# POOL interleaves its gathers and scatters in pairs in a mixture-of-experts kernel

## The reference

```python
x = x + 0.5 * ffn(layernorm(x))
x = x + attn(layernorm(x))
x = x + 0.5 * ffn(layernorm(x))

def ffn(h):                        # the part that the change touches
    probs = softmax(h @ gate_W.T)              # 8 experts
    top_v, top_i = top_k(probs, 2)             # each token takes two
    gates[t, top_i[t]] = top_v[t]
    out_e = (silu(h @ w1_e) * (h @ w3_e)) @ w2_e   # 128 -> 512 -> 128, for each expert
    routed = sum over e of gates[:, e] * out_e[e]
    shared = (mean over 8 small experts of the same form)
    return 0.5 * shared + 0.5 * routed
```

## Time and profile before

| | |
|---|---|
| median of 3 runs | 809.28 us |
| lowest, highest | 808.66, 810.8 us |
| span of the profiled execution | 936.1 us |
| mean granted clock of TensorE in it | 0.937 of full speed |
| PE busy | 733.7 us, 78% |
| POOL busy | 453.4 us, 48% |
| indirect DMAs | 144 fetches, 144 sends |

### The profile page before, as it was taken

One profiled execution on the slowest core, in us unless ns is written; L12 is line 12 of the kernel. 1 busy time (PEld: TensorE's weight loads), 2 busy tenths in 40 slices (PEclk: granted clock), 3 DMA queues, 4 the chain that ended last, 5 costly groups with the idle time before them and its releaser, 6 DMA issues. The chain is left out here.

```text
span 936.1 us, 16201 instructions
## 1 busy us (share of the span) xinstructions
PE 733.7 (78%) x4308; PEld 601.7 (64%) x4309; DVE 453.9 (48%) x1108; ACT 341.4 (36%) x889; POOL 453.4 (48%) x580
## 2 busy tenths in 40 slices
PE   4878979787878888937877689899878887978850
PEld 3757768676767676824654577687757666767740
DVE  7697633332233232426999847653324232333327
ACT  3514613323232332437764253633223233232320
POOL 6780054464535455358886240033554545546433
PEclk9979989998999999968999899999999999999985
DMA  9500010010111111031101000000110101111127
GB/s 329 173 1 1 1 35 29 29 39 28 39 28 34 34 34 34 26 98 47 45 24 35 23 23 1 1 23 24 32 37 28 39 28 39 34 34 36 31 68 224
DMA packets 45126, 43.68 MB, mean 47 GB/s; under 512 B 6048, under 2 KB 39840, under 8 KB 44704
## 3 DMA queue, kind: packets, MB, share of 16 engines
q1 hardware_dynamic: 31648, 22.22, 7.7%
q0 software_dynamic: 9216, 18.89, 7.3%
q10 hardware_dynamic: 4224, 2.10, 0.8%
HBM read 27.46 MB, written 15.73 MB: 46 GB/s over the span
## 5 line engine op out<-in xcount | busy, mean ns | idle before, releaser
L1073 ACT ACTIVATE silu<-psG 128x512 f32<-128x512 f32 x208 | 123.7, 596 | 330.4 <-PE psG L1206 210.1
L714 DVE TENSOR_TENSOR hr<-silu,psU 128x512 f32<-128x512 f32 x144 | 98.9, 687 | 282.5 <-ACT silu L1073 136.2
L1357 PE MATMUL psY<-W,hT 128*128 x1120 | 158.9, 287 | 26.9 <-issue 16.8
L602 POOL DMA_INDIRECT results<-yout,target_now x144 | 141.0, 979 | 63.9 <-issue 35.2
L583 POOL DMA_INDIRECT rows<-tokens,source_now x144 | 138.7, 963 | 58.6 <-issue 38.3
L1357 PEld LDWEIGHTS psY<-W,hT 128*128 128x128 f32 x1120 | 141.9, 199 | 38.2 <-issue 38.1
L1116 ACT ACTIVATE hT<-psH 128x512 f32<-128x512 f32 x144 | 85.9, 597 | 118.9 <-PE psH L1340 74.2
L1340 PE MATMUL psH<-ident,hr 128*128 128x128 f32 x576 | 89.7, 279 | 42.4 <-DVE hr L714 39.1
L1340 PEld LDWEIGHTS psH<-ident,hr 128*128 128x128 f32 x576 | 69.8, 142 | 73.2 <-ACT hT L1116 24.9
L1204 PE MATMUL psG<-W13H,xTH 128*128 x144 | 72.6, 504 | 15.4 <-issue 6.8
L579 POOL COPY source_now<-source 128x4 int32 (+1 forms) x36 | 7.0, 195 | 141.0 <-DVE source L866 117.7
(11 more groups left out here) (177 smaller groups left out, 1306.3 us busy)
## 6 DMA issues: line engine op xcount, KB each, us to landing
W<-w_e SPq DMA_DIRECT2D x3, 2048.0 KB, 13.8
tokens<-XN SPq DMA_DIRECT2D x16, 256.0 KB, 3.1
Y<-results SPq DMA_DIRECT2D x32, 128.0 KB, 2.2
YF<-results SPq DMA_DIRECT2D x16, 256.0 KB, 5.3
rows<-tokens,source_now POOLq DMA_INDIRECT x144
results<-yout,target_now POOLq DMA_INDIRECT x144
X<-x SPq DMA_DIRECT2D x8, 256.0 KB, 5.6
out<-X ACTq DMA_DIRECT2D x8, 256.0 KB, 2.6
```

The lines of the kernel that those rows point to most:

```text
L602: pool.indirect_dma_start(results, bass.IndirectOffsetOnAxis(ap=target_now[:, s.u, t:t + 1], axis=0), yout[:, s.u, t, :], None).then_inc(y ...
L714: dve.tensor_tensor(hidden, silu[:, s.u % 2, :], psU[:, s.u % 2, :], ALU.mult).then_inc(h_done, 1)
L1073: act.activation(silu[:, s.u % 2, :], psG[:, s.u % 2, :], ACT.Silu).then_inc(silu_done, 1)
L1357: i = pe.matmul(into[:, t * D:(t + 1) * D], hT[:, s.u % 2, f, :], W2[:, bass.ds(at + f * D, D)], start=(f == 0), stop=(f == FT - 1))
```

## The change

The two stages of POOL's pipeline are each cut in two halves, and the halves alternate. A step k is now: wait for `y_done` of group k - 3, copy its targets, two sends; wait for the buffer of group k, copy its sources, two fetches; the other two sends; the other two fetches. Nothing else in the kernel changes.

```diff
-                def fetch_rows(s):
-
-                    if s.past(2):
-                        wait_apart(pool, xT_psum, s.i + (l * GROUPS - 1))
-                    pool.tensor_copy(source_now[:, s.u, :], source[:, bass.ds(s.i * GT, GT)])\
-                        .then_inc(source_link, 1)
-                    wait_apart(pool, source_link, s.i + (l * GROUPS + 1))
-                    for t in range(GT):
-                        pool.indirect_dma_start(
...
-                pipelined(pool, [(fetch_rows, 0), (send_results, 3)], GROUPS, 2, guard=1)
+                def fetch_pair(half):
+                    def run(s):
+                        if half == 0:
+                            if s.past(2):
+                                wait_apart(pool, xT_psum, s.i + (l * GROUPS - 1))
+                            pool.tensor_copy(source_now[:, s.u, :], source[:, bass.ds(s.i * GT, GT)])\
+                                .then_inc(source_link, 1)
+                            wait_apart(pool, source_link, s.i + (l * GROUPS + 1))
+                        for t in range(half * GT // 2, (half + 1) * GT // 2):
+                            pool.indirect_dma_start(
...
+                def send_pair(half):
+                    def run(s):
+                        last = isinstance(s.i, int) and s.i == GROUPS - 1
+                        if half == 0:
+                            if not last:
+                                wait_apart(pool, y_done, s.i + (l * GROUPS + 1))
...
+                        for t in range(half * GT // 2, (half + 1) * GT // 2):
...
+                pipelined(pool, [(send_pair(0), 3), (fetch_pair(0), 0), (send_pair(1), 3), (fetch_pair(1), 0)],
+                          GROUPS, 2, guard=1)
```

More of the change, by code:

```diff
@@ L573, in _ @@
                 pool.wait_ge(table_done, l + 1)
-                def fetch_rows(s):
-                    if s.past(2):
-                        wait_apart(pool, xT_psum, s.i + (l * GROUPS - 1))
-                    pool.tensor_copy(source_now[:, s.u, :], source[:, bass.ds(s.i * GT, GT)])\
-                        .then_inc(source_link, 1)
-                    wait_apart(pool, source_link, s.i + (l * GROUPS + 1))
-                    for t in range(GT):
-                        pool.indirect_dma_start(
-                            rows[:, s.u, t, :], None, tokens,
-                            bass.IndirectOffsetOnAxis(ap=source_now[:, s.u, t:t + 1], axis=0))\
-                            .then_inc(rows_in[s.u], 16)
@@ L588, in send_results @@
[L588 to L604, removed]
@@ L606, in _ @@
-                pipelined(pool, [(fetch_rows, 0), (send_results, 3)], GROUPS, 2, guard=1)
+                def fetch_pair(half):
[8 more added lines that the diff above has]
+                            pool.indirect_dma_start(
+                                rows[:, s.u, t, :], None, tokens,
+                                bass.IndirectOffsetOnAxis(ap=source_now[:, s.u, t:t + 1], axis=0))\
+                                .then_inc(rows_in[s.u], 16)
+                    return run
@@ new lines, in send_pair @@
+                def send_pair(half):
[4 more added lines that the diff above has]
+                                wait_apart(pool, y_done, s.i + (l * GROUPS + 1))
+                            else:
+                                pool.wait_ge(y_sent[s.u], 16 * GT * (GROUPS // 2 * (l + 1) - 1))
+                            pool.tensor_copy(target_now[:, s.u, :], target[:, bass.ds(s.i * GT, GT)])\
+                                .then_inc(target_link, 1)
+                            wait_apart(pool, target_link, s.i + (l * GROUPS + 1))
+                        for t in range(half * GT // 2, (half + 1) * GT // 2):
+                            if last and t < GT - 1:
+                                pool.wait_ge(y_part, (GT - 1) * l + t + 1)
+                            elif last:
+                                pool.wait_ge(y_done, GROUPS * (l + 1))
+                            pool.indirect_dma_start(
+                                results, bass.IndirectOffsetOnAxis(ap=target_now[:, s.u, t:t + 1], axis=0),
+                                yout[:, s.u, t, :], None).then_inc(y_sent[s.u], 16)
+                    return run
```

## The result

The changed kernel takes 825.27 us (median of 4, 824.1 to 826.47) against 809.19 us beside it (4 runs): a ratio of 1.0193, 95% interval 1.0179 to 1.0208. It is 16.1 us slower. The forecast was 817, its range 804 to 827; the part of the range that belongs to the forecast's own mechanism was 813 to 825.

What follows compares the result with a forecast made beforehand. POOL did not look like a bound; PE's undisturbed steps gave 11.37 us per group. Per layer 0.5 + 14 x 0.23 = 3.7 us, 7.4 for two, called 8: 809.3 + 8 = 817 us, range 804 to 827.

Steps and rivals of the forecast that it cites:

- The disturbed profile: First profile of the kernel before: span 936.1 us, 127 us longer than the timed runs' median of 809.28.
- standstills: Idle stretches in routed stages while POOL fetches, 4 us per group; estimated to be hardly present in timed runs.
- T0: PE's time for a group of four tiles in the routed stages when nothing disturbs it: 11.37 us.
- The lead: Fetched rows were T0 = 11.4 us further ahead in the old order, covering POOL's lag of 3.2 us a layer.
- First lateness: Rows first fetched behind y_done reach PE 0.5 us late (0 to 1.0): wanted after 13.07 us, there after 13.5.
- The period, 11.60 us: Group period after the change, set by POOL's work from targets' copy to last fetch's end; 0.23 us over T0.
- The limit (b): Loop from y_done through fetched rows back to PE's transposes: two periods take 11.4 to 11.9 us each, 11.6 midway.
- Landing: Time from the last fetch's end on POOL until rows are there for PE: 1.2 to 2.2 us.
- upper bound of 16: Largest loss in the forecast's own sum, two layers: 2 x (1.0 + 14 x 0.49) = 16 us.
- The cover holds: First rival, 27%: POOL's steps are a little shorter in timed runs, and the time stays at 809 us.
- faster: Second rival, 13%: fetches in pairs with sends between break part of the standstills; halved, that gives 802.5 us.
- Much slower: Third rival, 8%: rows land late and POOL loses 0.24 us more per wait; period 12.0, loss 19.5, 829 us.

Runs made afterwards that it cites:

- e0_before: The kernel before, profiled again without an edit: 809.13 us in its one run, span 807.5 us.
- e1: The kernel before with only the order changed, no pairs: four sends of group k-3, then four fetches of k; 826.58 us against 809.58, ratio 1.0203.
- e2: The changed kernel with sends trailing by four groups in place of three, pairs kept; 809.97 us against 809.58 for the kernel before, ratio 1.0006.
- e5: The kernel before with one more POOL memset per group; 811.21 us against 809.74 without it, ratio 1.0016.
- e4: The changed kernel with one more POOL memset per group; 835.02 us against 809.74 for the kernel before, ratio 1.0309.
- e6: The changed kernel with padding rows fetching 2048 different tokens in place of token 0; 822.46 us against 809.74 for the kernel before, ratio 1.0147.
- e3: The changed kernel with POOL's loop written out, so its waits are for constants; 810.63 us against 809.58 for the kernel before, ratio 1.0013.

## Why the prediction was right in kind and half in size

- **The disturbed profile.** That timed runs do not have the standstills, and that T0 is 11.37, was an estimate; e0_before shows both: a span of 807.5 and periods of 11.37. What disturbed that one profiled execution is open. I expected the new profile to stay near 936 and to show no wait for rows: wrong, since the new execution was not disturbed and so showed the loss itself.
- **The lead is what the change spends.** Right: e1 has a loss as large without the pairs, e2 none with them. That POOL's pace costs nothing in the old order was an argument from the rows; e5 shows it with an instruction added.
- **First lateness, 0.5 us per layer.** It was 0. The transposes of group 3 stand 13.2 us after the end of `y_done`'s copy in both kernels (144.39 to 157.60 after). That step is unrolled on POOL, and with waits for constants its fetches end early. I had counted the loop's 0.81 there. The lateness came one group later: group 4, the first that the loop fetches, has a period of 11.88 and so stands 0.51 us behind its place.
- **The period, 11.60 us.** The term was mis-sized: 11.77, and 11.80 in layer 1. POOL's pace in the loop is 11.75. Of the difference, 0.04 is in the old order's own rows (11.64 from copy to copy where my rows held 11.60), and 0.1 comes with the pairs, as a DMA after one of the other kind takes 1.00 or 0.99 us in place of 0.97 or 0.94. Since the loss per group is a difference of two near numbers, 0.15 us more of pace raised it from 0.23 to 0.40, and 13 periods in two layers from 6 to 10.4 us (10.9 with layer 1's own).
- **The limit (b), the loop through `y_done`.** It was said to give 11.6 as well, and so close to POOL's pace it nearly is: POOL begins each group in the changed kernel 0.25 to 0.6 us after DVE's copy, and 0.25 is the distance where it waited. In two groups of layer 1 it held POOL back, by 0.23 and 0.32 us. It is the weaker of the two: e4's memset passed on at 0.26 us per period and not at half of its 0.28.
- **Landing, 1.7 us after the fetch.** Right for all groups but the last: PE begins 1.5 to 1.8 us after the end of a fetch. The rate's end in the earlier trace rows, 1.2 us, was too short for this, and so was the 2.15 us from a fetch's start by which the prediction had 815.7; measured from there it is 2.5 to 2.8.
- **The last group.** Missing from the sum: its rows land 3.1 us after the fetch and cost 1.8 us per layer, 3.6 of the 16.1. e6 takes 3.0 of it away in the rows by spreading the reads. The row that I used as the upper bound is of group 0, which holds no padding (why e6 begins there 1.8 us after the fetch and not 2.2 is open). The first profile had the sign: from 363 to 371 us, beside group 17's fetches, the POOL queue's 146 DMA packets took 38.4% of the 16 engines' time, and its 160 from 286 to 294 us took 14.0%.
- **Rivals.** *The cover holds* and *faster* are refuted by the result itself. *Much slower* named the size better (829) than the forecast but not the reason: rows of groups 4 to 16 did not land as late as in the earlier trace rows, and the period was 11.8 and not 12.0. The figure of 802.5 in the second rival should be 802.8 (809.3 less half of 13). POOL's wait for PE did not go altogether: one of 5.5 us is left, ahead of layer 1's group 2. My first rival's figure (POOL 4% quicker and nothing is lost) is the mechanism of e3, where POOL is 9% quicker and the loss all but vanishes.

The sum with measured terms: 5.2 + 5.6 for the 13 periods of the two layers and 2 x 1.8 for their last ones are 14.5 us, of 15.0 between the spans and 16.1 between the medians. So the mechanism was right and the forecast's 8 us held half of its cost: per layer it had 3.7 us for lateness and pace where the rows show 5.2 and 5.6, and nothing for the padding's 1.8. The result lies 0.3 us above the forecast's own 813 to 825. That the loss equals the upper bound of 16 in its sum is luck, as the terms of that bound (rows 1.0 us late, periods of 11.86) are not those that were measured. The last 0.5 to 1.6 us are not assigned; medians of before alone moved by 0.5 us between groups of runs.

## What to carry to other kernels

A queue slower than the engine that it feeds can be harmless, as long as its lag over a whole stage is smaller than its lead; both are to be read before its instructions are reordered. When a request is moved behind a wait for the consumer's results, the lead goes, and the queue's full pace becomes the period. If such an order is wanted, make the queue faster first: constants in the waits of an unrolled loop took 1.1 us of 11.75 off here. A comparison that comes out equal can still hide two differences, as e1 does: read its periods before calling the two kernels the same.

When a profile's span does not fit its timed runs, take the costs from its undisturbed stretches and profile once more.

## What the runs showed of the hardware

- Gathers whose 128 rows all name one 512-byte row of DRAM were slow: PE began 3.1 us after the last one's instruction on POOL ended, against 1.5 and 1.8 us when each gather's rows named some 29 tokens (e6).
- A wait on POOL through a register, after a copy on POOL itself, put 0.81 us between the copy and the DMA; with a constant it was 0.28 (e3).
- In the changed kernel an indirect DMA behind one of the other direction took 0.99 to 1.00 us on POOL, where one behind its own kind took 0.96 to 0.99: a gather 0.99 in place of 0.96, a scatter 1.00 in place of 0.98.
- Once in each layer POOL stood still for 2.03 us between two indirect DMAs in five of the traces, the first of before and e0 among them, and in the other five it did not. The cause is open.
